# Filler products at the head, an early ScalarE exponential, recurrence weights scaled later, and gate products in another order

## What is computed

```python
x = x + cross_attention(layernorm(x), ctx)          # 16 heads of 8
x = x + moe(layernorm(x))                           # 1 shared + 7 routed experts, top 2, hidden 352
n = layernorm(x)
c = attention(n, ctx) + attention(n, n, causal)     # source and target attention
h = lstm(concat(n, c), lstm_w, lstm_b)              # 64 steps, 128 units, gates i, j, f, o
x = x + relu(h @ ffn_w1 + b1) @ ffn_w2 + b2
x = x + top1_moe(layernorm(x))                      # 8 experts, capacity 320
```

## Time and profile before

| | |
|---|---|
| median of 3 runs | 740.86 us (739.43 to 752.29) |
| the profiled execution | 741.43 us, span 739.5 us |
| busy: PE, PEld, DVE, ACT, POOL | 91%, 77%, 59%, 47%, 18% of the span |
| chain that ended last | PE 78%, DVE 11%, issue 5%, ACT 2%, POOL 2%, DMA 1% |
| PE busy in 0 to 15 us | none |
| PE busy in 480 to 600 us (recurrence) | 120.00 of 120.00 us |
| experts of the last block | one every 6.1 us from 681.52 us on |

### The profile page before, as it was taken

How to read it: one execution, slowest core, us unless ns; L and a number is a source line. 1 busy time by engine, 2 the same in 40 slices (tenths; PEclk the granted TensorE clock), 3 DMA queues, 4 the chain that set the end, 5 groups by cost and what they waited for, 6 DMA issues and landing times.

```text
span 739.5 us, 16640 instructions
## 1 busy us (share of the span) xinstructions
PE 671.3 (91%) x6559; PEld 569.3 (77%) x6559; DVE 439.0 (59%) x1152; ACT 344.0 (47%) x930; POOL 133.2 (18%) x220
## 2 busy tenths in 40 slices
PE   1799999999999999989999998999999999796992
PEld 0477778988889888867676676899999999543772
DVE  5499857748746657679899998233343444410221
ACT  0489852333222222357788786355554544101331
POOL 4425740010000000024000010000000000062576
PEclk9999999999999999989999999999999999788997
DMA  7500300000000000123322100000000000213222
GB/s 258 171 18 20 132 3 1 1 1 1 1 1 1 1 0 1 48 66 77 83 66 67 36 7 2 1 2 2 1 2 2 1 1 2 58 40 90 18 21 20
DMA packets 30006, 24.46 MB, mean 33 GB/s; under 512 B 3825, under 2 KB 27122, under 8 KB 29554
## 3 DMA queue, kind: packets, MB, share of 16 engines
q1 hardware_dynamic: 26482, 21.40, 10.0%
q0 software_dynamic: 3456, 2.12, 2.1%
HBM read 17.96 MB, written 5.80 MB: 32 GB/s over the span
## 4 chain that ended last, share of the span: by engine, by line
PE 78%; DVE 11%; issue 5%; ACT 2%; POOL 2%; DMA 1%; POOLq 0%; DVEq 0%; SPq 0%; ACTq 0%
PE SC L665 15%; PE PT L675 12%; PE MI L594 5%; PE SC L844 5%; PE PT L584 5%; PE SC L575 3%; PE SC L933 3%; PE SC L765 3%; PE SC L804 2%; PE PJ L551 2%; DVE kexp L1216 2%; PE SC L768 2%; PE SC L809 2%; PE SC L771 2%; PE PT L815 2%
## 5 line engine op out<-in xcount | busy, mean ns | idle before, releaser
L1048 ACT ACTIVATE big<-SC 128x512 f32<-128x512 f32 x88 | 52.6, 599 | 144.3 <-PE SC L665 144.3
L675 PEld LDWEIGHTS PT<-wd,big 128*128 128x128 f32 (+1 forms) x768 | 90.2, 191 | 2.5 <-issue 0.4
L675 PE MATMUL PT<-wd,big 128*128 128x128 f32 (+1 forms) x768 | 90.6, 274 | 0.0
L1378 DVE TENSOR_TENSOR big<-SC,big 128x512 f32<-128x512 f32 (+1 forms) x88 | 60.5, 689 | 41.7 <-PE SC L665 32.4
L665 PE MATMUL SC<-xP,wgP 128*128 128x512 f32 x264 | 78.8, 407 | 0.7 <-DVE big L1378 0.3
L665 PE MATMUL SC<-xP,wuP 128*128 128x512 f32 x264 | 74.4, 390 | 0.0
L594 PEld LDWEIGHTS MI<-vblk,PTs 128*64 128x64 f32 x1536 | 50.1, 140 | 11.7 <-ACT oT L998 2.8
L594 PE MATMUL MI<-vblk,PTs 128*64 128x18 f32 x1536 | 54.5, 214 | 4.7 <-ACT big L1003 1.7
L665 PEld LDWEIGHTS SC<-xP,wuP 128*128 128x128 f32 x264 | 49.6, 188 | 10.9
L993 ACT ACTIVATE PTs<-PT 128x512 f32<-128x512 f32 x96 | 52.3, 595 | 6.6 <-PE PT L584 5.5
L584 PE MATMUL PT<-ident,sc 128*128 128x128 f32 x384 | 53.6, 284 | 0.6 <-ACT sc L988 0.6
(11 more groups left out here) (223 smaller groups left out, 1331.5 us busy)
## 6 DMA issues: line engine op xcount, KB each, us to landing
kvs<-in_ctxT SPq DMA_DIRECT2D x32, 64.0 KB, 1.9
w1s<-in_e1w SPq DMA_DIRECT2D x8, 256.0 KB, 2.8
w2s<-in_e1w SPq DMA_DIRECT2D x8, 256.0 KB, 3.3
wg<-in_wg SPq DMA_DIRECT2D x1, 1408.0 KB, 8.9
wu<-in_wu SPq DMA_DIRECT2D x1, 1408.0 KB, 11.9
slots_in<-big SPq DMA_DIRECT2D x1, 1300.0 KB, 6.0
big<-slots_in SPq DMA_DIRECT2D x8, 130.0 KB, 2.4
wd<-in_wd SPq DMA_DIRECT2D x2, 512.0 KB, 13.9
```

What stands on the lines that cost most here:

```text
L675: last = pe.matmul(PT[:, e % 2, t * P:t * P + P], h[0:w, t * P:t * P + P], wd[0:w, e, c, :], start=(c == 0), stop=(c == 2))
L1048: act.activation(sg[a % 2], SC[:, a % 2, :], ACT.Silu).then_inc(s["silu_done"], 1)
L1378: last = dve.tensor_tensor(hT[e % 2][0:w, c, :], SC[0:w, 2 + a % 2, :], sg[a % 2][0:w, :], ALU.mult)
```

## The change

Six edits in one.

1. **Head, PE:** 18 filler products (bf16, 128x512, result unused) as soon as `warm` is cleared, 8 more after the eighth Newton step, and 2 after the second, third and fourth group of turns. POOL clears `warm` first, ahead of the 2600-column `zeros`.
2. **Head, ACT:** an exponential of one column once `zeros` is cleared, ahead of everything else.
3. **Folded weights:** they are made from the unscaled `lw` as soon as it has landed; ACT's copy of each becomes three instructions (128, 128 and 256 columns), two of them with scale 0.5. POOL scales `lw` and `f1` after the splits of the mixture of experts.
4. **Second attention:** `pv` stands ahead of `proj` in step 1 alone. The last four tiles are turned one by one into PJ[:, 384:512] in steps 8 to 11, ahead of `proj`, each copied by one ACT instruction of 128 columns in steps 9 to 12; PE waits for them in step 13.
5. **Recurrence:** step 0 has no `gate_in` but two more fillers; steps 1 and 2 have two each. ACT's copies follow.
6. **Burst:** `BURST` is 28 instead of 20, in the same loop of 4.

```diff
-BURST = 20
+BURST = 28
-LAST_ROWS = 9
+LAST_ROWS = 8
...
+            pool.memset(warm[:, :], 0.0).then_inc(s["warm_ready"], 1)
             pool.memset(zeros, 0.0).then_inc(s["zero_ready"], 1)
...
-            link(pool.memset(warm[:, :], 0.0))
...
             pool.sem_inc(s["prep_done"], 1)
-
-            pool.wait_ge(s["lstm_w_loaded"], 16 * N_LSTM)
-            scaled(lw[:, :, 0:P], 0.5)
-            scaled(lw[:, :, 2 * P:4 * P], 0.5)
-            scaled(lw[:, 2, :], 0.5)
-            scaled(f1[:, :], 0.5)
-            pool.sem_inc(s["prep_done"], 1)
...
             pool.wait_ge(s["late_w_loaded"], 16 * N_LATE)
+            pool.wait_ge(s["fold_done"], 2)
+            pool.wait_ge(s["lstm_w_loaded"], 16 * N_LSTM)
+            scaled(lw[:, :, 0:P], 0.5)
+            scaled(lw[:, :, 2 * P:4 * P], 0.5)
+            scaled(lw[:, 2, :], 0.5)
+            scaled(f1[:, :], 0.5)
+            pool.sem_inc(s["prep_done"], 1)
             pool.wait_ge(s["ln_evacuated"], 2 * GRP + 1)
...
+            pe.wait_ge(s["warm_ready"], 1)
+            keep_warm(SC[:, 0, :], 18)
+            pe.wait_ge(s["ln_newton"], 8)
+            keep_warm(SC[:, 0, :], 8)
             pe.wait_ge(s["consts_loaded"], 16 * N_CONST)
...
                 rows_turned(q, TPB[q % 2])
+                if q:
+                    keep_warm(SC[:, 1, :], 2)
...
             proj(0, 0, 0, 0)
-            pe.wait_ge(s["prep_done"], 2)
+            pe.wait_ge(s["lstm_w_loaded"], 16 * N_LSTM)
             pe.matmul(PT[:, 0, :], wat[:, 4, :], lw[:, 1, :], start=True, stop=True).then_inc(s["fold_done"], 1)
...
                 if known(m, BIAS_COLS):
+                    pe.wait_ge(s["prep_done"], 2)
                     pe.wait_ge(s["kexp_ready"], n + 3)
...
+                if known(m, 1):
+                    pv(n - 1, 1 - p, (v - 1) % 4)
+                if isinstance(m, int) and 0 <= m - LAST_ROWS < 4:
+                    pe.wait_ge(s["kexp_ready"], n + 3)
+                    pe.wait_ge(s["ln_xn"], 3 * GRP)
+                    pe.transpose(PJ[:, 384:512], xn_last[:, m - LAST_ROWS, :], ident[:, :])
                 if not known(m, NU1 - 3, NU1 - 2, NU1 - 1):
                     proj(2 - p, n + 3, i + 1 + p, 1 - p)
-                if known(m, LAST_ROWS):
-                    pe.wait_ge(s["ot_copied"], n - 1)
-                    rows_turned(3 * GRP - 1, MI)
+                if known(m, LAST_ROWS + 5):
                     pe.wait_ge(s["ln_evacuated"], 3 * GRP)
-                if not known(m, 0):
+                if not known(m, 0, 1):
...
-                if t == 0:
-                    gate_in(1, 0)
-                if j < BLK - 1 and more > 0:
+                if t in (1, 2):
+                    gate_in(1, 2 * t - 2)
+                    gate_in(1, 2 * t - 1)
+                elif t == 0:
+                    keep_warm(PT[:, 0, :], 2)
+                elif j < BLK - 1 and more > 0:
                     gate_in(k + 1, j + 1)
...
+            act.wait_ge(s["zero_ready"], 1)
+            act.activation(rs[0][:, 0:1], zeros[:, 0:1], ACT.Exp)
             act.wait_ge(s["prep_done"], 1)
...
-                act.activation(lwo[n][:, :], PT[:, n, :], ACT.Copy).then_inc(s["fold_copied"], 1)
+                act.activation(lwo[n][:, 0:P], PT[:, n, 0:P], ACT.Copy, scale=0.5)
+                act.activation(lwo[n][:, P:2 * P], PT[:, n, P:2 * P], ACT.Copy)
+                act.activation(lwo[n][:, 2 * P:4 * P], PT[:, n, 2 * P:4 * P], ACT.Copy, scale=0.5
+                               ).then_inc(s["fold_copied"], 1)
...
+                if isinstance(m, int) and 0 <= m - LAST_ROWS - 1 < 4:
+                    o = (11 + m - LAST_ROWS) * P
+                    act.wait_ge(s["proj_done"], n + 3)
+                    last = act.activation(xnT[:, o:o + P], PJ[:, 384:512], ACT.Copy)
...
-                        if t == 0:
-                            g_copy(1, 1, 0)
-                        if j < BLK - 1 and more - kp > 0:
+                        if t in (1, 2):
+                            g_copy(1, 1, 2 * t - 2)
+                            g_copy(1, 1, 2 * t - 1)
+                        elif 0 < t and j < BLK - 1 and more - kp > 0:
```

15 lines of the change are left out of this document (7 added, 8 removed).

## The result

| | before | changed kernel |
|---|---|---|
| median of 20 runs | 742.86 us (739.04 to 752.68) | 739.78 us (737.76 to 742.23) |
| ratio, 95% interval | | 0.9961 (0.9945 to 0.9976) |
| the profiled execution | 741.43 us, span 739.5 | 740.06 us, span 738.0 |

The change gains 0.39%, 2.9 us (1.8 to 4.1). Foretold were 6.05 us and 734.8: the direction is right, the size is half, and the measured median lies above the range (730.7 to 739.3). Of the 5.0 us between 734.8 and 739.78, 2.0 are the starting point: the prediction took 740.86 for the kernel before, from three runs, and twenty give 742.86.

The account below looks back on a forecast made before the run. PE was taken to bound the kernel, busy for 91% of the span and holding 78% of the last chain. The terms -3.0 - 2.0 - 0.6 + 1.05 - 1.5 = -6.05 us gave a median of 734.8, range 730.7 to 739.3.

Parts of the forecast that it names:

- Head: Start of the kernel: faster normalising and full clock, less a wait for the context tile; -3.0 us, between -1.4 and -3.8.
- DVE's 1.4: Head: 16 normalisations take 4.5 us instead of 5.92 without POOL's scaling, counted together with ACT's table load; 1.4 us less.
- the clock's 2.4: Head: if fillers bring 2.4 GHz, turns save 0.5, two projections 0.7 each, scores 0.47; together 2.4 us.
- 0.8 back for the context tile: Head: the third projection waits for its context tile, landing between 27.1 and 28.4; 0 to 0.9 us lost, 0.8 taken.
- the head stays at half clock: Rival, head: fillers don't bring full clock, so the head gives only 1.4 us and the time is 736.4; chance 0.20.
- Step 1 of the second attention: Second attention: `pv` fills PE's 1.43 us wait for the keys; -2.0 us, between -1.3 and -3.2.
- its 1.8 us: Second attention, step 1: turned probabilities start at 325.8 instead of 327.65 as `pv` fills the wait; 1.8 us.
- Last rows: Second attention, step 9: turns stay but the 0.69 us wait for ACT goes; -0.6 us, between -1.3 and +0.2.
- Recurrence start: Steps 0 to 2: step 0 gets shorter, steps 1 and 2 each gain a `gate_in` and a wait; +1.05 us, +0.3 to +1.3.
- Burst: Fillers before the first expert: 32 more bring it full clock but end 0.7 us late; -1.5 us, between 0 and -2.2.
- The rival's half of x: Rival, burst overruns: x us at half clock add x/2 of lateness; 743.6 us at x = 20; chance 0.04.
- Clock elsewhere: Rival: shifted work changes which stretch falls to half clock; full clock at 640 to 644 saves at least 2.0, 732.5; chance 0.12.

Follow-up runs that it names:

- no_first18: The changed kernel without the 18 fillers at its very start; 740.6 us, ratio 0.9959 to the kernel before.
- warm_alone: The changed kernel plus 15 fillers in three PE waits at the head; 740.56 us, ratio 0.9972 to the kernel before.
- wd_later: The changed kernel with SP issuing context tiles 2 and 3 ahead of the down weights, 4 and 5 between them; 735.62 us, ratio 0.9884.
- before_again: The kernel before, unchanged, run again for a second trace; 740.85 us, span 738.8.
- three: The changed kernel with SP's context tiles ahead of and between the down weights, BURST = 24, gate products as one, one, two; 733.91 us, ratio 0.9869.
- gates_back: The changed kernel with block 1's four gate products as before (two in step 0, one each in steps 1 and 2); 737.54 us, ratio 0.9912.
- warm_no18: The changed kernel with SP's tiles earlier, BURST = 24, gate products one, one, two, 15 fillers in head waits, without the first 18; 734.25 us, ratio 0.9874.

## Why the prediction was wrong

The distances by the code that stands in the stretch (us; traces in brackets). There are 18 traces; the first row takes those with SP's queue and the fillers as in the change (over all 13 with the 26 first fillers it is 20.62), and the second leaves out no_first18 (22.10) and warm_alone (19.76).

| stretch | old code | changed code | improved |
|---|---|---|---|
| start to first projection | 22.44 (3) | 20.72 (6) | |
| first projection to mark 4 | 20.24 (3) | 21.46 (6) | SP's order 19.89 (2); with the 15 fillers as well 18.62 (5) |
| marks 18 to 20 | 10.04 (3: 9.35 to 10.61) | 7.91 (10), 11.17 (3) | 7.91 (2) |
| marks 20 to 28 | 36.31 (3) | 35.05 (15) | |
| mark 48 to h products of t = 3 | 22.6 (3), 23.7 to 23.8 (2) | 23.6 (2), 24.5 to 24.8 (5) | 22.6 (3), 23.5 and 25.4 (3) |
| t = 3 to burst start | 172.4 (5) | 172.83 (7) | |
| burst start to second expert's w2 | 38.30 (5) | 37.90 (7: 35.9 to 39.7) | 24 a pass: 36.13 (6) |

In the row of marks 18 to 20 the higher figure of the changed code is that of traces in which the clock fell there; in all three of the old code it fell. In the row of mark 48 the clock falls in every trace, for 3.4 us in the lower figures and for 6.8 in the higher; in two of the improved traces 6.8 us go with 23.5 and in one 10.2 us with 25.4.

**Head: the step that failed.** Foretold -3.0, as the sum of DVE's 1.4, the clock's 2.4 and 0.8 back for the context tile. Measured over the traces: 1.7 us up to the first projection, of which 1.2 is given back by mark 4, so **-0.5**. The first part is as I worked it out (0.5 for the turns and 1.4 for DVE). What failed is the rest, in three points.

First, I took from the earlier trace rows that before runs at half clock until 31 us; in the second trace of before it was full from 26. So part of the 2.4 was never there to be won, and the trace that I worked from was the worst of three.

Second, I let the late tile cost 0.8: I had it landing by 28.4 at the latest, 4.3 us after its issue, and it took 5.7 to 6.3 us and let PE start between 28.8 and 29.9, after waits of 2.5 to 3.7 us (seven traces). On the path that is 1.2 to 1.6 us (21.46 against 20.24 in wd_later and 19.89 in the mean of both traces with SP's new order), since without it PE waits 1.35 us for DVE instead.

Third, I added the clock as if once risen it stayed. In the nine traces of the changed head without fillers in the waits PE was busy for 4.4 to 5.6 of the 10 us from 20 to 30, and the clock fell between 28.4 and 31.6 us. In all six with the 15 fillers PE was busy for 7.8 to 8.9, and it held, also in the one where the tile was late. (The old head lost the clock once in three traces, at 32.7 us in before_again.) So wd_later and warm_alone show that the tile and the clock are two losses, not one. With both cured the way from the first projection to mark 4 takes 18.62 us, 1.6 less than before, where I had counted 1.9 for the clock: the gain that I saw was there, but the changed kernel didn't keep it.

The rival "the head stays at half clock" failed, as the first projection is at full clock in every trace. The 18 first fillers are lost, as it said: the first projection starts at 20.72 and 20.75 us without them and at 20.16 to 21.09 with them. In the first trace the recorded clock is full from 6.9 us, falls at 10.3, when PE has been idle since 8.1, and is full again from 17.2. The Trainium skill (TensorE: Matmul & The Clock Gate, Part 1) says that an idle PE goes back to half rate; the traces agree for the 18. At 30 us they show more, a fall where PE was idle only in pieces, in two traces (wd_later, three) of no more than 1.5 us each.

**Step 1 of the second attention.** -2.0 foretold; -1.4 measured, as a mean of two cases: -2.1 where the clock holds and +1.1 where it falls at 317 to 320 us (3 of 13). The wait did go, but it isn't where most of the gain comes from, so the nearness of -2.1 to -2.0 is in part luck. In before_again marks 19 to 20 take 3.73 us. The turns and scores ahead took 1.75 and 1.16 us there against 1.04 and 0.69 at full clock, 1.2 more, which covers DVE's wait of 1.06. By an estimate from these numbers the old order at full clock would thus take 2.7 us, where the new order takes 2.29: 0.4 us for the order, about 1.7 for the clock. The order may well be what keeps the clock: the old one lost it 9.9 to 11.5 us after mark 17 in all three traces, the new one there in none of ten. The three falls of the new one come 5.6 to 5.8 us after mark 17, ahead of the moved products, and the old one could have them too. The sum read its 1.8 us off rows at half clock and had no case of a loss.

**Last rows.** -0.6 foretold, -1.26 measured, the lower end of its range: the turns do fall into waits, and ACT's smaller copies aren't felt.

**Recurrence start.** +1.05 foretold, +1.0 measured at equal clock. It was the one edit that the rows spoke against, and gates_back confirms it.

**Burst: the second step that failed.** -1.5 foretold; -0.4 measured, between -2.4 and +1.4. What failed is that PE's issuing was taken as steady. After 20 to 22 us of fillers it stops for 1.5 to 2.4 us in 8 of 13 traces with 96 or 112 fillers, and in none of 5 with 80, which are done by then; the trace of before couldn't show it. In the three traces with 112 and no stop the term is -2.4 to -1.2, in the mean -1.7, the size foretold; in the four with one it is 0.0 to +1.4. With 96 fillers the stop falls into the wait for the rows. The sum's other input, x, the time at half clock at the burst's start, was 2.7 to 5.1 us by the recorded clock with 112 fillers, and not 2.5. The rival's half of x is borne out: 35.88, 36.81 and 37.05 us at 2.7, 4.6 and 5.1 us without a stop. The old burst has the same x (2.8 to 5.9), so this moves both sides.

**Clock elsewhere.** The rival gave it 0.12 and only as a gain (its time should read 732.8, which is 734.8 less its 2.0). It was a loss: 0.4 us in the routing stretch (172.83 for 172.4, with turns at 1.12 for 0.66), and about 0.3 more in 449 to 465 us, where the clock was at half for 6.8 us rather than 3.4 in 5 of 7 traces for 2 of 5. Whether the earlier fall in the routing belongs to the changed start of the recurrence, as 7 against 5 traces suggest, or to chance, stays open; of the six traces with one, one, two gate products, two have 172.8 and four 172.4.

The sum of what was measured: -0.5 - 1.4 - 1.26 + 1.0 + 0.3 + 0.4 - 0.4 = -1.9, at the small end of the timed interval (-1.8 to -4.1). One reason for that is on record: the two traced executions of before took 741.43 and 740.85 us, against medians of 742.0 to 745.5, so what its longer executions lose stands in no trace. In those the mean granted clock is lower: 0.950 to 0.964 in its executions of 745 to 748 us beside the experiments, against 0.964 to 0.974 in those below 743. The prediction's range was too narrow because each term had a bound for its mechanism, but none for where the clock would stand in the trace of before and of after. Its upper end, 739.3, was also below the 739.7 that its own upper ends add up to.

**The best version.** Edits 1 to 4 kept, the gate products as one, one, two, `BURST = 24`, context tiles ahead of the down weights, and 22 fillers in waits: 733.01 us, 0.9877 (0.9857 to 0.9897) of before, 9.1 us less. The 18 fillers can go. What the 22 fillers add isn't shown by the times: without them the ratio was 0.9869 (0.9822 to 0.9915), and only the traces tell the two apart, by 0.9 us at the head.

## What to carry to other kernels

A faster stage doesn't keep its clock if its waits stay: put fillers into the waits between its products, not ahead of the stage (0.9 us in the traces here, too little for these times to show), and ask what transfer it will now run into. Before an estimate rests on a half-clock stretch of one trace, look at a second trace of the same kernel; distances between fixed events show at once what is program and what is a draw. Size a burst so that it ends just ahead of what it waits for: overrun costs in full, the clock held over a wait of 1.86 us (three), and a wait of 3.43 us lost it (warm_no18).

## What the runs showed that I had not expected

- SP's queue: three weight issues took 11.5 us of SP while the gate and up weights were ahead of them, and 0.44 us each when issued after 25 us. A 64 KB tile behind them landed 5.75 us after its issue, 2.0 us in the median of all tiles.
- The recorded clock: it reads 1.00 from the start until its first change, although products ran at half pace (1.91 us for a folded product at 23.72 in before_again, 1.02 at full clock in the changed kernel). What a product takes tells it, the record doesn't.
- The rise isn't fixed to the work: with the same 26 fillers it came between 15.2 and 18.6 us. The Trainium skill (TensorE: Matmul & The Clock Gate, Part 1) says of the rise that it varies from run to run; these traces agree, and the falls vary too.
- The stop in the burst, 1.5 to 2.4 us: its cause wasn't found, and it doesn't show as a wait. It goes with the time and not with the number of fillers: in seven of the eight traces the last filler ahead of it starts 21.2 to 21.4 us after the first, with 87 to 92 fillers out (counted back from the end), fewer where more of them ran at half clock; in the eighth it comes at 19.8 us. POOL's last scatter ends 21.1 to 21.2 us after the first filler. It does so in the traces without a stop as well, so a link to it isn't shown.
